# The first sequence's k pieces on VectorE, and the one-hot rows of the stacks later

## What is computed

```python
nesting, segments = _syntax_info(token_ids)            # scans over the token ids
h = concat([pos_emb, nest_table[nesting], seg_table[segments]], -1) @ W     # (32, 512, 128)
q, k, v = split((layernorm(h) @ qkv_w.T + qkv_b).reshape(b, s, 8, 3, 16))   # 8 heads of 16
attn = softmax(einsum('bshc,bthc->bhst', q, k) / sqrt(16))
h = h + einsum('bhst,bthc->bshc', attn, v).reshape(b, s, 128) @ out_w.T + out_b
h = h + ffn(layernorm(h))        # softmax gate less a threshold, relu(fc1), lora_A, lora_B, fc2
```

## Time and profile before

| | |
|---|---|
| time, median of 3 runs | 1123.27 us (1123.06 to 1123.34) |
| the profiled execution's own time | 1124.57 us |
| its span, first to last instruction | 1122.8 us |
| busy: TensorE, VectorE | 1040.9 us (93%), 923.4 us (82%) |
| busy: ScalarE, GpSimd | 819.2 us (73%), 721.5 us (64%) |
| mean granted TensorE clock | 0.957 of full |
| 128x512 row maxima on VectorE (L1039) | 1024 of 678 ns |
| pieces on GpSimd (L486, L480, L503) | 64 each of 1157, 1159, 1156 ns |

### The profile page before, as it was taken

How to read it: one execution, slowest core, us unless ns; L and a number is a source line. 1 busy time by engine, 2 the same in 40 slices (tenths; PEclk the granted TensorE clock), 3 DMA queues, 4 the chain that set the end, 5 groups by cost and what they waited for, 6 DMA issues and landing times.

```text
span 1122.8 us, 20355 instructions
## 1 busy us (share of the span) xinstructions
PE 1040.9 (93%) x6158; PEld 408.6 (36%) x6158; DVE 923.4 (82%) x2410; ACT 819.2 (73%) x1610; POOL 721.5 (64%) x716
## 2 busy tenths in 40 slices
PE   5378899999999999999999999999999999999955
PEld 3012234433434434333334334333433443333322
DVE  7498888889988898888988889888998889888111
ACT  2317787878877888788877788787877788777731
POOL 1865667787666776677666677678666777622332
PEclk8558999999999999999999999999999999999986
DMA  2554545555555455555554455655555445541110
GB/s 69 149 134 94 130 108 142 129 128 132 137 128 125 121 130 130 138 121 135 137 129 122 126 123 129 142 124 128 136 137 129 124 122 124 127 103 44 51 49 30
DMA packets 93530, 132.43 MB, mean 118 GB/s; under 512 B 18205, under 2 KB 69918, under 8 KB 87398
## 3 DMA queue, kind: packets, MB, share of 16 engines
q1 hardware_dynamic: 91872, 129.54, 47.9%
q10 hardware_dynamic: 1550, 1.59, 0.5%
HBM read 89.20 MB, written 35.01 MB: 111 GB/s over the span
## 4 chain that ended last, share of the span: by engine, by line
PE 66%; DVE 17%; DMA 7%; ACT 4%; issue 3%; POOL 1%; SPq 1%; POOLq 0%; ACTq 0%
PE pv L751 17%; PE mix L764 16%; PE sc L738 13%; DVE negmax L1039 9%; PE mix L818 8%; DMA den_dram<-ctx_sb 3%; PE mix L801 3%; DVE bn L1029 2%; PE mix L823 2%; ACT probs L600 2%; DVE h L1065 2%; PE mix L839 2%; DMA den<-den_dram 2%; PE mix L783 1%; PE mix L776 1%
## 5 line engine op out<-in xcount | busy, mean ns | idle before, releaser
L1039 DVE TENSOR_REDUCE negmax<-mix 128x1 f32<-128x512 f32 x1024 | 648.7, 678 | 61.4 <-PE mix L764 61.0
L600 ACT ACTIVATE probs<-sc 128x512 f32<-128x512 f32 x1024 | 556.9, 601 | 116.2 <-PE sc L738 112.3
L738 PE MATMUL sc<-qstk,kstk 120*128 120x512 bf16 x1024 | 363.2, 381 | 5.3 <-ACT probs L600 4.6
L764 PE MATMUL mix<-kstk,qstk 96*128 96x512 bf16 x1024 | 330.3, 393 | 25.7 <-DMA kstk<-stack_dram 7.6
L751 PE MATMUL pv<-probs,vals 128*32 128x512 f32 x2048 | 244.8, 595 | 0.0
L531 POOL TENSOR_TENSOR ctxh<-ctx_sb,rdenb 128x512 f32<-128x512 f32 x64 | 80.8, 1267 | 183.7 <-DMA rdenb<-rden_dram 101.8
L764 PEld LDWEIGHTS mix<-kstk,qstk 96*128 96x128 bf16 x1024 | 89.4, 98 | 266.7 <-issue 82.2
L738 PEld LDWEIGHTS sc<-qstk,kstk 120*128 120x128 bf16 x1024 | 99.8, 98 | 106.3 <-ACT probs L600 33.3
L818 PE MATMUL mix<-xn2T,fc1T_sb 128*128 128x512 f32 x256 | 137.7, 620 | 0.7 <-ACT hid L659 0.7
L509 POOL TENSOR_TENSOR qk<-qk,rstdb 128x512 f32<-128x512 f32 x64 | 81.1, 1269 | 67.6 <-DMA rstdb<-rstd_dram 67.6
L751 PEld LDWEIGHTS pv<-probs,vals 128*32 128x32 f32 x2048 | 59.1, 109 | 117.4 <-issue 100.1
(11 more groups left out here) (142 smaller groups left out, 1114.6 us busy)
## 6 DMA issues: line engine op xcount, KB each, us to landing
stack_dram<-pieces SPq DMA_DIRECT2D x192, 128.0 KB
rdenb<-rden_dram SPq DMA_DIRECT2D x64, 256.0 KB
qstk<-stack_dram SPq DMA_DIRECT2D x31, 384.0 KB, 6.5
kstk<-stack_dram SPq DMA_DIRECT2D x31, 384.0 KB, 8.6
rstdb<-rstd_dram SPq DMA_DIRECT2D x32, 256.0 KB, 3.4
wrow<-w_dram SPq DMA_DIRECT2D x32, 256.0 KB
out<-out_sb SPq DMA_DIRECT2D x32, 256.0 KB, 4.9
qstk<-stack_dram SPq DMA_DIRECT2D x31, 256.0 KB, 6.8
```

The lines of the kernel that those rows point to most:

```text
L600: act.activation(probs[:, c % 8, i % 2], sc[:, i % RING], ACT.Exp).then_inc(s_exp, 1)
L738: pe.matmul(sc[:, i % RING, :], kstk[0:KROWS, u, h, j * P:(j + 1) * P], qstk[0:KROWS, u, h, :], start=True, stop=True).then_inc(s_score, 1)
L764: pe.matmul(max_bank(m), qstk[0:STK, u, h, j * P:(j + 1) * P], kstk[0:STK, u, h, :], start=True, stop=True).then_inc(s_mxmm, 1)
L1039: dve.tensor_reduce(negmax[:, m // NT, m % NT:m % NT + 1], max_bank(m), AX.X, ALU.max, negate=True).then_inc(s_max, 1)
```

## The change

The second piece, residual and third piece of k of sequence 0 are no longer made by GpSimd, which makes those of q alone for that sequence, but by VectorE, in step -3 ahead of slot 8. VectorE waits for each of GpSimd's three q operations first, so that the semaphores count in the old order. ScalarE's 24x4096 copy of the one-hot rows moves from step -4, slot 13 (ahead of the v copy and of the first pieces of sequence 0) to step -3, slot 8 (behind those pieces, ahead of `copy_rT` of sequence 1 and `copy_v` of sequence 1). The three DMAs that copy these rows to the other buffers move to step -2, slot 8, behind the first pieces of sequence 1 and ahead of `copy_rT` of sequence 2.

```diff
--- before.py
+++ after.py
@@ -547,9 +547,9 @@
                 "scale": lambda b, u, side: scale(b, side),
                 "v": lambda b, u, _: value(b, u),
                 "finish": lambda b, u, _: finish(b),
-                "residual": lambda b, u, side: residual(b, side),
-                "second": lambda b, u, side: second(b, side),
-                "third": lambda b, u, side: third(b, side),
+                "residual": lambda b, u, side: residual(b, side) if b or not side else None,
+                "second": lambda b, u, side: second(b, side) if b or not side else None,
+                "third": lambda b, u, side: third(b, side) if b or not side else None,
                 "norm2": lambda b, u, _: norm2(b, u),
                 "add_bias": lambda b, u, _: add_bias(b, u),
                 "normalise": lambda b, u, _: normalise(b, u),
@@ -588,6 +588,8 @@
             def fill_heads():
                 act.copy(kstk[STK:KROWS, 0, :, :],
                          const_sb[STK:KROWS, 4:4 + NH].unsqueeze(2).broadcast_to([3 * NH, NH, S])).then_inc(s_const, 1)
+
+            def copy_heads():
                 act.wait_ge(s_const, 4)
                 for u in range(1, U):
                     act.dma_start(kstk[STK:KROWS, u, :, :], kstk[STK:KROWS, 0, :, :]).then_inc(s_heads, 16)
@@ -674,8 +676,10 @@
 
             def step(t, u):
                 for c in range(SLOTS):
-                    if t == -4 and c == 13:
+                    if t == -3 and c == 8:
                         fill_heads()
+                    if t == -2 and c == 8:
+                        copy_heads()
                     for place in range(3):
                         for name, ahead, part in [w[2:] for w in ACT_WORK if w[:2] == (c, place)]:
                             if runs(t + ahead):
@@ -1034,6 +1038,17 @@
                 for j in range(NT):
                     dve.bn_aggr(mv[:, j, :], bn[:, j, :]).then_inc(s_mv, 1)
 
+            def first_k_pieces():
+                dve.wait_ge(s_pc0, 2)
+                dve.wait_ge(s_pc1, 1)
+                dve.tensor_tensor(pieces[:, 1, 1, :], qk32[:, 1, :], pieces[:, 1, 0, :], ALU.subtract).then_inc(s_pc1, 1)
+                dve.wait_ge(s_res0, 1)
+                dve.tensor_tensor(qkr[:, 1, :], qk32[:, 1, :], pieces[:, 1, 0, :], ALU.subtract).then_inc(s_res0, 1)
+                dve.wait_ge(s_pc1, 2)
+                dve.wait_ge(s_res0, 2)
+                dve.wait_ge(s_pc2, 1)
+                dve.tensor_tensor(pieces[:, 1, 2, :], qkr[:, 1, :], pieces[:, 1, 1, :], ALU.subtract).then_inc(s_pc2, 1)
+
             def row_max(b, m):
                 upto(dve, s_mxmm, b, 32, m + 1)
                 dve.tensor_reduce(negmax[:, m // NT, m % NT:m % NT + 1], max_bank(m), AX.X, ALU.max,
@@ -1140,6 +1155,8 @@
                         copy_weights()
                     if t == -4 and c == 7:
                         cut_folded()
+                    if t == -3 and c == 8:
+                        first_k_pieces()
                     for place in range(3):
                         for name, ahead, part in [w[2:] for w in DVE_WORK if w[:2] == (c, place)]:
                             if runs(t + ahead):
```

## The result

The changed kernel is slower: 1126.88 us median of 19 runs (1123.2 to 1129.79), beside 1123.14 for the kernel before in as many (1122.06 to 1128.76). Its profiled span is 1126.3 us, 3.5 more than before. The forecast was 1123.0.

What follows compares the result with a forecast made beforehand. VectorE's row maxima were taken to set the pace, their start bound by the fill's chain of waits. SyncE's earlier issue gave -0.24 us, every other part 0; off the 1123.27 median, 1123.0 us, range 1122.2 to 1124.3.

Steps and rivals of the forecast that it cites:

- The three copies of the one-hot rows ... Cost 0: Copies behind sequence 1's first pieces on ScalarE, 49.90 to 52.3 us: 0 for those queued behind, 0 as traffic.
- VectorE alone sets the pace once the maxima run: From VectorE's first row maxima, begun by 56 us: shifting their start moves everything behind by as much.
- Rival 3: ScalarE's queue: issuing the three copies beside SyncE takes 4.8 us, not 2.40; VectorE loses about 1.7: 1124.7; chance 0.05.
- The cover that I counted there: ScalarE's rT copy of sequence 2, at 52.3 to 52.6, precedes TensorE's waiting max product with 0.4 us left.
- 1.0 us of cover (1.1 forecast): ScalarE's rT copy of sequence 1, 38.3 to 38.6, precedes SyncE's rstd store, due about 39.7, by 1.1 us.
- The hold: VectorE's k subtractions and GpSimd's q steps take turns; VectorE ends 0.54 us after GpSimd; chance 0.62 together with rival 5.
- rival 1: GpSimd is held by VectorE's subtractions, q's third ends at 39.35: loss 0.76 us, so 1124.0; chance 0.14.
- rival 2: Neither VectorE nor GpSimd is held during the k subtractions: 1122.8 us; chance 0.14.
- the forecast gain of 0.24 us: On SyncE, k's second piece is issued at 39.00 instead of 39.24, and the rstd store and first product move with it.
- rival 5: SyncE's rstd store lands no sooner with two 128 KB stores close ahead: no change, 1123.3; within the forecast's 0.62 chance.
- The clock (rival 4): TensorE's clock rises later than 91 to 92 us; shares chance 0.05 with an unseen DMA alignment.
- the forecast's 0.22 us for each microsecond: Cost of a later TensorE clock rise; over 10 us later would be needed for 2.25 us.

Runs made afterwards that it cites:

- late_full: Kernel before with k's pieces on VectorE, fill and first copies in their old place, the three full copies made a second time at the late place: 1.0025.
- late_small: As late_full, but the three repeated copies move only 24 x 16 elements each: 1.0004 to the kernel before.
- copies_later: Changed kernel with the three copies moved from step -2 to step -1, slot 8: 1.0009 (0.9994 to 1.0025) to the kernel before.
- bias_first: Changed kernel with GpSimd's bias of sequence 2 put ahead of its two scale steps in step -1: 1.0006 to the kernel before, 0.9998 when run again.
- before_bias_first: Kernel before with GpSimd's bias of sequence 2 put ahead of the scale steps in step -1: 0.9994 (0.9978 to 1.0009).
- k_only: Kernel before with only sequence 0's k pieces moved to VectorE, one-hot rows filled and copied in their old place: 1.0004 (0.9993 to 1.0015).
- after_again: The changed kernel, unaltered, measured a second time: 1.0024 (1.0013 to 1.0034) to the kernel before, median 1126.57 us.

## Why the prediction was wrong

The range was missed by one step, "The three copies of the one-hot rows ... Cost 0". I asked of their traffic only by when each transfer in flight was due (16 tiles of slack, 86 us), and of their issue only who waits behind ScalarE. I didn't walk the queue that runs beside it. Behind the k half on SyncE stand the ids, five pieces, and the rstd store of sequence 2, whose load releases GpSimd's scale and, behind that, the bias step that VectorE comes for with 0.77 us in hand. Nor was it right that VectorE alone sets the pace once the maxima run: ahead of each h_sb it must meet GpSimd's bias step of the sequence in front. In the kernel before that meeting had 0.77 us in hand for sequence 3 and 1.16 to 4.35 us for the next eight, so it was tight just where the copies were put. The four links are each shown: copies to SyncE (late_full against late_small and copies_later), SyncE to the rstd load (8.3 to 9.0 us from k half to rstd store in the six profiles with all three full copies there, 6.1 to 6.4 in the six with none, and no other input of that store late), load to bias step (rows of GpSimd above), bias step to VectorE (bias_first).

Rival 3 had the place, the three copies issued while SyncE issues, but the wrong victim, and its 1.7 us are under the 2.4 us by which the pair came late. ScalarE's issues took 2.41 us, as before, and rT of sequence 2 was copied at 50.87, released by TensorE, not by ScalarE's queue. The cover that I counted there was real; the uncovered side was the other one.

The other steps, point by point:

- ScalarE: k's first piece ended at 34.19, 3.94 us after the scale's start, as worked out. rT of sequence 1 ran at 37.84 and its store at 39.10, 1.0 us of cover (1.1 forecast).
- The hold: VectorE's three subtractions took 1.55, 1.64 and 1.58 us instead of 0.69. k's second ended 2.81 us after the start of q's second (2.80 forecast). GpSimd's q third took 1.42 instead of 1.15, a hold of 0.27 (0.25 forecast), its v step 1.71. So the two engines take turns, and rival 1 and rival 2 are both out. "SBUF — State Buffer" of the Trainium skill, section "Who interferes with whom", says so of a VectorE instruction with two SBUF inputs beside a GpSimd instruction that reads SBUF; these rows agree (1.55 to 1.64 us for 0.69, 1.42 for 1.15).
- The rstd store of sequence 1, counted from the start of q's second: 5.12 or 5.13 us in all eleven profiles with k on VectorE, 5.36 or 5.37 in the three without. That is the forecast gain of 0.24 us.
- It was mostly given back at the next link, as rival 5 had it, so as a gain of the whole the 0.24 us was wrong too: the store took 2.35 us to land, not 2.16 (41.45 less 39.10, before 42.07 less 39.91), and k's third piece was issued 7.88 us after q's second began, against 7.93. So the first half of the change is worth 0.05 us at that point, too little for any time here to show. The first maximum then varies, 15.52 to 16.36 us after q's second, in kernels that are alike up to there (the kernel before and before_bias_first, one program so far, have 16.19 and 15.66), so that the 49.49 of the one profile isn't a gain that can be counted on; k_only has 16.16.
- The clock (rival 4): the granted clock averaged 0.88 from 90 to 91 us in the kernel before and 0.74 from 92 to 93 in the changed one, with 0.50 ahead of it and 1.00 behind. So it rose some 2.3 us later, behind work that came 2.4 us later, and cost nothing of its own. In after_again it rose only near 94, some 1.3 us more; at the forecast's 0.22 us for each microsecond that is about 0.3 us, an estimate.

What stays open: the loss doesn't stay at 2.42 us behind the pair of maxima. At VectorE's inversions of the denominators (32 of them, L1073, from 128.14 us on) the changed kernel's profile is 0.99 us behind that of the kernel before at the first, 2.07 at the 18th, 4.07 at the last, and 3.5 at the end of the span. In after_again it is 3.25 behind at the first and 2.35 at the last. The executions of either kernel spread over more than 6 us, and I take this for that spread, which no run here takes apart. Nor do the runs show what it is in a running copy that holds SyncE's next issue. "DMA: Bandwidth & Descriptors" of the Trainium skill, section "Issuing engines are not separate DMA queues", says that DMAs of different engines run on the same 16 DMA engines and interleave. The trace agrees: from 51 to 52 us of the changed kernel ScalarE's queue took 51% of the 16 engines' time and SyncE's 41%. That the issue instruction itself waits is only in the rows here.

## What to carry to other kernels

When a DMA is moved, write down, for the time in which it will run, the issues on every other queue, and follow the last of them to the engine that sets the pace; the deadline of the moved DMA and the slack of the transfers in flight are not enough. An engine that "sets the pace" still has to meet others: look for the operation whose input comes with less than a microsecond to spare, since a late side chain enters there. An engine that comes sooner to such a meeting only waits longer. And two operations of one list that don't need each other, one of which waits for a DMA (scale, then bias), are better the other way round: here it cost nothing that the times show (0.9994 in the kernel before) and took the late DMA off the path.

## What of the hardware I had not expected

A DMA being issued can stretch when another queue's transfer runs: single issues on SyncE of 0.49 to 0.58 us took 1.36 to 1.94 us beside copies of 24 rows of 8 KB from SBUF to SBUF. It wasn't in proportion to the bytes: one copy of 192 KB cost SyncE's queue 1.9 us, three cost 2.3 to 3.0 (six profiles, 8.31 to 9.01 against 6.06), and three of 24 x 16 elements 0.6. Which instruction stretches varies from one execution to the next.
